# Four temporal-tap copies of each pair of groups moved from ScalarE to GpSimd

## The reference, cut to what matters

```python
# 1. graph convolution, then four branches of 8 channels; b1 and b2 are 5-tap convolutions over time
y = relu(bn(Wgc @ (x + x_agg)))
b1 = bn(tconv(relu(bn(Wb1 @ y)), Wt1, d=1)); b2 = bn(tconv(relu(bn(Wb2 @ y)), Wt2, d=2))
b3 = bn(maxpool3(relu(bn(Wb3 @ y))));        b4 = bn(Wb4 @ y)
x = relu(concat(b1, b2, b3, b4) + res)
# 2. attention over the 400 tokens of an image, softmax of exp(-|Q-K|^2)
t = t + softmax(exp(-dist2(Q, K))) @ V       # Q, K, V from the layer-normed t
# 3. a recurrence over the 400 tokens: y_t = sigmoid(BN(W t)_t + V y_{t-1})
t = t + scan(...)
```

## Time and profile before

| | us |
|---|---|
| median of 3 runs | 223.04 (221.67 to 223.66) |
| the profiled execution's own time | 221.07 |
| its span, first to last instruction | 219.2 |
| busy: PE / ACT / DVE / POOL | 193.8 / 170.3 / 160.7 / 29.8 |

### The profile page before, as it was taken

How to read it: one execution, slowest core, us unless ns; L and a number is a source line. 1 busy time by engine, 2 the same in 40 slices (tenths; PEclk the granted TensorE clock), 3 DMA queues, 4 the chain that set the end, 5 groups by cost and what they waited for, 6 DMA issues and landing times. The chain is left out here.

```text
span 219.2 us, 3489 instructions
## 1 busy us (share of the span) xinstructions
PE 193.8 (88%) x1171; PEld 98.4 (45%) x1171; DVE 160.7 (73%) x298; ACT 170.3 (78%) x323; POOL 29.8 (14%) x44
## 2 busy tenths in 40 slices
PE   6858999999999969699999999999999998479950
PEld 6633646546546435323243343434333423259840
DVE  0649369999999944996876695968777795675990
ACT  4073799699699799988988989899999974286740
POOL 7000000370150080260203010101010000000000
PEclk9999999999999999969999999999999999997995
DMA  6940200276349150591534435170800000000016
GB/s 176 374 154 21 74 2 0 49 273 165 88 167 240 41 224 22 213 228 31 134 100 123 108 81 147 40 189 4 212 14 3 0 0 0 0 3 3 0 67 235
DMA packets 20213, 21.95 MB, mean 100 GB/s; under 512 B 2046, under 2 KB 17086, under 8 KB 20068
## 3 DMA queue, kind: packets, MB, share of 16 engines
q1 hardware_dynamic: 20196, 21.73, 33.8%
HBM read 14.74 MB, written 6.96 MB: 99 GB/s over the span
## 5 line engine op out<-in xcount | busy, mean ns | idle before, releaser
L507 ACT ACTIVATE arena<-ps 128x800 f32<-128x800 f32 (+1 forms) x56 | 44.6, 798 | 5.8 <-PE ps L1064 5.4
L514 ACT ACTIVATE arena<-arena 128x800 f32<-128x800 f32 (+1 forms) x56 | 46.4, 830 | 0.0
L1064 PE MATMUL ps<-qa,ka 128*128 128x400 bf16 (+1 forms) x128 | 35.5, 341 | 2.0 <-ACT arena L507 1.9
L1064 PE MATMUL ps<-qb,kb 96*128 96x400 bf16 (+1 forms) x128 | 35.5, 339 | 0.0
L741 DVE TENSOR_TENSOR psum<-arena 128x400 f32<-128x400 f32 x32 | 19.6, 611 | 14.2 <-ACT arena L514 14.2
L741 DVE TENSOR_TENSOR psum<-psum,arena 128x400 f32<-128x400 f32 x32 | 19.5, 608 | 6.1 <-ACT arena L514 4.7
L1064 PEld LDWEIGHTS ps<-qa,ka 128*128 128x128 bf16 (+1 forms) x128 | 10.4, 98 | 26.2 <-ACT arena L507 13.7
L1097 PE MATMUL ps<-arena,vb 128*32 128x400 f32 x192 | 21.6, 525 | 0.3 <-issue 0.3
L750 DVE RECIPROCAL arena<-ps 128x400 f32<-128x400 f32 x7 | 18.5, 2649 | 0.0
L1182 PE MATMUL ps<-yb,cst 128*128 128x120 f32 (+1 forms) x102 | 16.6, 309 | 1.7 <-ACT yb L597 1.4
L660 DVE COPY arena<-arena 32x400 f32<-32x400 f32 x48 | 17.2, 358 | 0.9
(11 more groups left out here) (151 smaller groups left out, 353.8 us busy)
## 6 DMA issues: line engine op xcount, KB each, us to landing
ka<-dk SPq DMA_DIRECT2D x32, 100.0 KB
qa<-dq SPq DMA_DIRECT2D x32, 100.0 KB
dk<-arena SPq DMA_DIRECT2D x8, 300.0 KB, 2.2
dq<-arena SPq DMA_DIRECT2D x8, 300.0 KB, 2.7
arena<-x_tok SPq DMA_DIRECT2D x4, 400.0 KB
t<-x SPq DMA_DIRECT2D x1, 1600.0 KB, 11.3
kb<-dk SPq DMA_DIRECT2D x16, 100.0 KB
qb<-dq SPq DMA_DIRECT2D x16, 100.0 KB
```

Source lines behind the costliest of these rows:

```text
L507: nc.scalar.activation(prob[par][:, lo:hi, :], ps[:, o:o + hi - lo, 0:N], ACT.Exp, scale=2.0).then_inc(e1_done, 1)
L514: nc.scalar.activation(p, p, ACT.Exp).then_inc(p_ready, 1)
L1064: last = mm_(ps[row:row + keys, bank, 0:N], kk[par][0:rows, b, o:o + keys], qq[par][0:rows, b, :], start=first, stop=not first, skip_group ...
```

## The change

The four copies of a pair that ScalarE made (taps 2 and 3 of branch 1, for both groups) are made by GpSimd, in a new function `tap_inputs(i)` of its program. The semaphore `u_act` becomes `u_pool`. GpSimd's program is unrolled, and its order is now: `tap_inputs(0)`, `tap_inputs(1)`, `square_parts(0)`, `tap_inputs(2)`, `square_parts(1)`, `tap_inputs(3)`, `square_parts(2)`, `square_parts(3)`, and only then `values(0)` and `values(1)`. VectorE's and TensorE's programs are the same but for the semaphore's name.

```diff
-            square_parts(0)
+            def tap_inputs(i):
+                if i > 1:
+                    pool.wait_ge(e_ready, i - 1 + CREDIT1)
+                for par in range(2):
+                    pool.wait_ge(zp_ready, 2 * i + par + 1)
+                    for k in POOL_TAPS:
+                        last = nc.gpsimd.tensor_copy(*tap_input(par, 1, k))
+                    last.then_inc(u_pool, 1)
+                pool.wait_ge(u_pool, 2 * i + 2)
+
+            tap_inputs(0)
+            for i in range(PAIRS):
+                if i < PAIRS - 1:
+                    tap_inputs(i + 1)
+                square_parts(i)
             for par in range(2):
                 values(par, par)
-            with pool.Fori(1, PAIRS) as i:
-                square_parts(i)
...
                 for par in range(2):
-                    act.wait_ge(zp_ready, 2 * i + par + 1)
-                    for k in ACT_TAPS:
-                        last = nc.scalar.copy(*tap_input(par, 1, k))
-                    last.then_inc(u_act, 1)
                     z_part(par, 96, P, ACT.Identity).then_inc(plain_ready, 1)
...
                         if j:
-                            pe.wait_ge(u_act, 2 * i + par + 1)
+                            pe.wait_ge(u_pool, 2 * i + par + 1)
```

More of the change, by code:

```diff
@@ L180, in build @@
             sem(n) for n in ("zeroed", "abs_done", "dve_c", "act_c", "pe_c", "mlo_ready", "prep_done", "bn_ready"))
-        (v_mixed, y0_ready, mixed, y_ready, branched, zp_ready, mx_ready, u_ready, u_act, pooled, tapped, ts_ready,
+        (v_mixed, y0_ready, mixed, y_ready, branched, zp_ready, mx_ready, u_ready, u_pool, pooled, tapped, ts_ready,
          t0_ready) = (
             sem(n) for n in ("v_mixed", "y0_ready", "mixed", "y_ready", "branched", "zp_ready", "mx_ready",
-                             "u_ready", "u_act", "pooled", "tapped", "ts_ready", "t0_ready"))
+                             "u_ready", "u_pool", "pooled", "tapped", "ts_ready", "t0_ready"))
         (centered, sq_ready, var_done, ln_ready, rstd_ready, xl_ready, kq_done, k1_ready, q1_ready, rk_ready,
@@ L253, in slot @@
             return (par * UNITS + u) % 2
-        ACT_TAPS = (2, 3)
+        POOL_TAPS = (2, 3)
         def tap_input(par, j, k):
@@ L658, in tap_inputs @@
                         for k in range(len(OUTER)):
-                            if j == 0 or k not in ACT_TAPS:
+                            if j == 0 or k not in POOL_TAPS:
                                 last = nc.vector.tensor_copy(*tap_input(par, j, k))
```

## The result

The changed kernel takes 230.82 us (median of 4 runs, 229.99 to 231.19), the kernel before 222.35 (4 runs, 220.5 to 223.66): a ratio of 1.038, with a 95% interval of 1.033 to 1.043. It is 8.5 us slower. The profiled execution has a span of 229.4 us, 10.2 more than that of before.

The account below looks back on a forecast made before the run. The prediction took a chain through VectorE's tap stretch and TensorE to set the turn, with ScalarE's copies outside it. 0 + 6.4 + 2.9 = 9.3 us on 223.04 gave 232 us, range 226 to 239.

Parts of the forecast that it names:

- Part 1: Tap copies leaving ScalarE, 2.1 us per pair, only lengthen its wait for VectorE's add in each turn: gain 0.
- Part 2: Four tap copies on GpSimd, 0.50 to 0.52 us each, are done before TensorE needs them: no cost by itself.
- Part 3: GpSimd's copies slow VectorE's tap stretch by 1.6 us a pair, at 0.78 us per us of GpSimd work: 6.4 us.
- Part 4: At the start of the attention TensorE waits for `vb`, since `values` stands behind all entropy parts: 2.9 us.
- A: Rival: GpSimd is starved through VectorE's tap stretch and TensorE's second product stalls: 239.5 us, chance 0.13.
- B: Rival: only the `values` wait counts, copies cost VectorE under 0.3 us a pair: 226 to 227 us, chance 0.15.
- C: Rival: neither contention nor wait, GpSimd gives way: 222.7 to 224.3 us, no change, chance 0.06.
- D: Rival: faster, ScalarE being the bound after all: 219 us, chance 0.03.

Follow-up runs that it names:

- experiment 3: Kernel before with ScalarE's 16 tap copies left out and made by no one: 222.29 us, ratio 1.0015 to the kernel before.
- experiment 7: Kernel before with one more tap copy of branch 1 moved from VectorE to ScalarE: 221.39 us, ratio 1.0008 to the kernel before.
- experiment 8: Kernel before with four idle GpSimd copies a pair behind VectorE's last tap copy, beside its PSUM instructions: 221.98 us, ratio 1.0006 to the kernel before.
- Experiment 2: Kernel before with only GpSimd's order changed, both `values` behind `square_parts(3)`: 227.03 us, ratio 1.020 to the kernel before.
- experiment 9: Experiment 2 with 14 idle TensorE products ahead of its first wait for `vb`: 225.26 us, ratio 1.014 to the kernel before.
- experiment 1: Changed kernel with both `values` back behind `square_parts(0)`, tap copies still on GpSimd: 224.82 us, ratio 1.013 to the kernel before.
- experiment 6: Experiment 1 with GpSimd writing zeros in place of its tap copies: 223.92 us, ratio 1.006 to the kernel before.
- experiments 3 to 7: Includes 4, experiment 1 with GpSimd's copies made twice, 229.87 us, and 5, experiment 1 with ScalarE keeping the first group's copies, 222.62 us.

## Why the prediction came out

The time, 232 against 230.8, is nearer than its terms. Two of them were off, one up and one down, and that they nearly cancel is luck.

- **Part 1, ScalarE's copies are worth nothing: shown,** by experiment 3 for the relief and by the 3.28 us wait in the profile after. What the prediction said beside it, that ScalarE has time to spare, holds only for giving it less: experiment 7 found none when it was given more.
- **Part 2, the copies are in time: shown.** Undisturbed, a GpSimd copy takes 0.51 to 0.52 us (experiment 8), the 0.50 to 0.52 taken from the 128x384 row. Beside VectorE's copies it took 0.54 to 0.56, and the first of a pair 0.8 to 0.9, since it waited for the maximum. TensorE's tap products never waited for GpSimd in a turn.
- **Part 3, the contention: the mechanism right, the size wrong.** The term was 4 x 1.6 = 6.4 us; it measured 4 x 0.89 = 3.6 in the trace and 2.9 in the runs. The step that failed is the ratio of 0.78 us lost per us of GpSimd's work. In the earlier trace rows operations of 0.86 to 1.16 us cost VectorE 0.65 to 0.75 each (one cast of the two took 1.10 us, the subtractions 1.22 and 1.31), in the profile after copies of 0.54 to 0.56 cost 0.21 to 0.23 each. That is a subtraction and not a ratio. In both places the slow VectorE instruction ends later than GpSimd's by its own length less 0.14 us: 0.22 for the copies, 0.23 for the casts, 0.43 for the subtractions (0.57 alone) of the earlier trace rows. So VectorE waits in full, and what it loses is GpSimd's length less the first 0.14 us, and less the time that VectorE had free anyway: 0.15 us of the 0.37 in which its copies follow each other, 0.06 of the 0.49 of the subtractions. That gives 0.51 - 0.29 = 0.22 and 0.86 - 0.20 = 0.66, where 0.22 and 0.65 were measured. A ratio scaled down to short instructions charges the fixed part as well. The forecast turn of 19.3 us was therefore 18.6, and VectorE's copies had none at 0.8 us.
- **Part 4, `values` behind the entropy parts: the mechanism right, the size low.** The term was 2.9 us with an upper bound of 3.9. Experiment 2 has 3.7 in the trace and 4.5 (3.4 to 5.5) in the runs, the changed kernel 4.2. The wait was 2.5 to 3.2 us as forecast. What I had only in the bound, a stretch at the lower clock longer than without the wait, came in all three traces that have the wait and no idle products: 0.5 us in experiment 2 and 1.7 in the changed kernel, by the sums under experiment 9.
- **The rivals.** A (GpSimd starved, 239.5 us) is out: GpSimd came in after every VectorE copy. B (only the wait counts) is out by experiment 1, whose interval starts at 1.009. C and D are out by the result.
- **The sum** of the two costs measured apart is 2.9 + 4.5 = 7.4 us, for 8.5 measured and 9.3 forecast.

On the sharing of ports, the Trainium skill's page SBUF — State Buffer ("Who interferes with whom") says that VectorE contends with GpSimd in two-port modes and, where GpSimd reads SBUF, with two SBUF inputs, and not with one SBUF input outside such a mode. The runs agree on each: copies slow beside copies (0.59 for 0.36) and beside plain writes (experiment 6), two-input maxima slow beside copies (0.77 and 0.88 for 0.57), a maximum and a write beside each other both at their own pace (0.56 and 0.42), and PSUM with one SBUF input not slow (experiment 8). It also says that the loser waits for the whole instruction. The ends of the instructions agree with that, to the 0.14 us. What the prediction made of it, 4 x 0.50 = 2.0 us a pair, was too much all the same (0.89 was measured): it charged each GpSimd copy from its start, and the VectorE copy beside it began 0.2 us later and had some time free.

## What to carry to other kernels

Before an engine is relieved, find its wait further on in the same turn: if it ends on another engine, the relief only makes it longer, and yet that wait doesn't say how much the engine could take on earlier. Work moved to GpSimd has two prices that its own short busy time doesn't show: each of its instructions holds up one of VectorE's SBUF copies beside it (here 0.22 us a copy), and everything behind it in GpSimd's one queue moves too, here the `values` that TensorE needed next, which cost more than the copies. A stall of TensorE should be priced at its full length, and the lower clock that comes with it added: here 0.5 to 1.7 us more than the kernel lost to the clock anyway. Compare the granted clock of the same stretch first: the entry of the attention differs by 1.5 us between traces with the same work and no wait.

## What the runs showed of the hardware

- GpSimd and VectorE alternate instruction by instruction: with 32x400 f32 copies on both, each starts one every 0.60 us. A VectorE copy lasts 0.59 us instead of 0.36, a GpSimd copy 0.54 to 0.56 instead of 0.51 to 0.52. Whichever comes second ends later than the other by its own length less 0.14 us: a VectorE copy by 0.22, a VectorE 128x400 subtraction by 0.43, a GpSimd copy by 0.38.
- GpSimd's writes alone hold up VectorE's copies as its copies do: 32x400 memsets cost them 0.69 us for three, copies 0.89 for four. A memset and a two-input maximum beside each other both kept their pace (0.42 and 0.56 us).
- With a wait of 2.5 to 3.2 us TensorE's granted clock was at its lower level for 6.8 to 10.2 us (three traces). The stretch of 6.8 us cost 2.0 us. At the same place without the wait it was there for 3.4 us, at a cost of 1.5 us (the kernel before, experiments 1 and 8), or not at all (experiments 3 to 7).
- In executions of kernels that are the same up to there, the first turn begins up to 2.9 us apart (21.96 us in the kernel before, 24.83 in experiment 2), by when the first DMA lands and whether a stretch of lower clock falls into them.
